# A transformer kernel with routed experts on one Trainium2 core: row transfers, pair rows and weight loads issued at other places

## The chip, the cores and the metric

The kernel runs on one core of a Trainium2 chip. TensorE (PE) multiplies matrices, VectorE (DVE) and ScalarE (ACT) work on rows, GpSimd (POOL) computes small things and issues indirect transfers, SyncE (SP) issues all other transfers. The metric is the device time of one execution in microseconds (us), lower is better.

## The reference

Two layers, each of a cross-attention and a mixture of eight experts, on 16 sequences of 128 tokens with 128 features. Everything is float32.

```python
x = x + jnp.tanh(g_xattn[0]) * _L0_xattn_ref(_layernorm(x, axis=-1), ctx_512, Wq, Wkv, Wo)
x = x + jnp.tanh(g_ffn[0]) * _L0_ffn_ref(_layernorm(x, axis=-1), gate_w, w1, w2)
x = x + jnp.tanh(g_xattn[1]) * _L1_xattn_ref(_layernorm(x, axis=-1), ctx_512, ctx_512, Wq, bq, Wk, bk, Wv, bv, Wo, bo)
x = x + jnp.tanh(g_ffn[1]) * _L1_ffn_ref(_layernorm(x, axis=-1), Wr, br, W1, b1, W2, b2, gamma, beta)
```

The attention has 16 heads of 8 features, 128 queries and 77 keys for each sequence. The feed-forward picks for each token the two experts (128 to 512 to 128 features, gelu in layer 0, relu in layer 1) with the largest gate logits and weights their outputs by a softmax of the two. Layer 1 adds biases and a layer norm with gamma and beta.

## The kernel before

Each engine has its own program, written out by hand; semaphores named in ONE and PAIR tie them together, and each engine goes through its program strictly in the order of the code. A layer has four parts: the attention loop, a tail with the routing, an expert loop of 39 tiles of 128 rows, and what follows.

**The attention loop** runs over steps s = 0 to 17. Sequence b is in flight over several steps: in step s the engines prepare sequence s (normalise, `xn`), make the queries of s-1, take the maxima and exponentials of b2 = s-2, and finish b3 = s-3 (weighted values, division, output projection, residual). Sequences are also handled in pairs, (0,1), (2,3) and so on, named by their second, odd member: for pair b4 = s-4, in odd steps, the rows of the updated x are normalised again for the experts ("pair rows", `xfa`), turned by PE, and give the gate logits; three to five steps later the routing has placed them, and POOL sends each sequence's rows to their two experts by two indirect transfers (`scatter(b, j, (k,))`, k = 0 and 1): sequence j = 0 of pair b8 = s-8 in odd steps, j = 1 of pair b9 = s-9 in even ones. So steps 9 to 15 have two transfers each, and steps 5 and 7 handle a pair without any transfer. 

What a step does, engine by engine, where the change and the prediction touch it (names as in the code and the trace):

- DVE: `maxima(b2)`, two TENSOR_REDUCE mx<-banks that follow PE's four score matmuls in pairs; the parts of the maxima (mxp); `divided(b3)` (RECIPROCAL); statistics of sequence s+2; `residual(b3)`; statistics of a pair (fmv); routing.
- PE: lower scores of b2 (they wait for the second exponential of the step before), values and weights of b3, queries of s-1, the turned maxima, scores of b2 (room,kz) with `less_max` (room,less), the turned xn, `project(b3)`, `turn_rows(b4)` (MATMUL banks<-ident,xfa, an odd step's only, waits for the pair rows), then `upper_scores(b1)` (MATMUL banks<-kz,room 32x324), on which DVE's next maxima wait.
- ACT: queries (q_s), `normed(s)` (xn<-x,rstd, waits for POOL's rstd), a copy of the turned maxima, `normalised(b4)` (xfa<-x,frs, odd steps), four exponentials (`exps`, ACTIVATE room<-banks 128x384), the copy xnT.
- POOL: `deviations(b4)` (frs, odd steps), in layer 1 half of the sum of expert outputs for sequence s+3 (x<-ob,x), the deviations rstd of the next two sequences (even steps), `counted`, and then the step's two scatters.

In layer 0, SP's `load_rest()` issues 256 KB weight loads, two per step, for all four weight tensors: wa1 and wa2 (layer 0's) in steps with sequence 0 to 7, wb1 and wb2 (layer 1's) with 8 to 15, and 15 small loads (`late_rows`) in between. The expert loop's row loads (`load_tiles`) come after that on the same queue.

Of the kernel before, what the change touches and what calls it, by code (L numbers as in the profile page):

```python
# [29 lines left out]
B = 16  # L30
# [6 lines left out]
E = 8  # L37
# [80 lines left out]
def pipeline(eng, n, lead, deep, step):  # L118

    for s in range(n + deep):  # L120
        step(Step(s))


def build(nc, a, out):
    ctx = ExitStack()
    with ctx:  # L126
# [296 lines left out]
        def _(sp):  # L423
            def load(dst, src, key):
                sp.dma_start(dst, src).then_inc(ld[key], 16)
# [13 lines left out]
            def load_rest():  # L439
                w1_, w2_ = a["L0_ffn_w1"], a["L0_ffn_w2"].rearrange("e (c p) d -> e p c d", p=P)  # L440
                w3_, w4_ = a["L1_ffn_W1"].rearrange("e (c p) d -> e p c d", p=P), a["L1_ffn_W2"]
                blocks = lambda w, e: w[:, e * F:(e + 1) * F].rearrange("p (c d) -> p c d", c=FC)
                pieces = ([lambda e=e: load(wa1[:, e * F:(e + 1) * F], w1_[e], "wa1") for e in range(E)]
                          + [lambda e=e: load(blocks(wa2, e), w2_[e], "wa2") for e in range(E)]
                          + [lambda e=e: load(blocks(wb1, e), w3_[e], "wb1") for e in range(E)]
                          + [lambda e=e: load(wb2[:, e * F:(e + 1) * F], w4_[e], "wb2") for e in range(E)])
                def late_rows():
                    with nc.allow_non_contiguous_dma(reason="two biases of 128 numbers, reordered"):
                        for dst, src in LATE:
                            load(dst, src, "w1")  # L450

                for c in range(B):
                    layers[0]["mx"].wait(sp, Step(c))
                    pieces[2 * c]()
                    layers[0]["ex"].wait(sp, Step(c))
                    pieces[2 * c + 1]()
                    if c == B // 2:
                        late_rows()

            def attention():  # L460
                S = layers[1]
# [4 lines left out]
                        sp.dma_start(ob[s.slot(UN)][:, k, :], o_dram[0][k * NTOK + c * T:k * NTOK + (c + 1) * T, :])\  # L466
                            .then_inc(s_ob[s.slot(UN)], 16)

            def load_tiles(l):
                S = layers[l]  # L470
                hear(sp, f"rowsT{l}")
                for r in range(2):
                    sp.wait_ge(s_sc[r], SC_LAYER * (l + 1))
                sp.wait_ge(s_zero, 16 * E)
                row = sp.alloc_register(f"row{l}")

                def tile(t):
                    S["xt"].wait(sp, t.back(UN))
                    apart(sp)
                    S["id"].wait(sp, t.back(UN))  # L480
                    apart(sp)
                    sp.reg_load(row, r_row[0:1, bass.ds(t.at(1), 1)])
                    r = sp.snap(row, min_val=0, max_val=E * REGION - P)
                    sp.dma_start(xg[t.slot(UN)][:, :], xg_dram[bass.ds(r, P), :]).then_inc(s_xg[l][t.slot(UN)], 16)
                pipeline(sp, NT, UN, 0, tile)

            hear(sp, "rows")
            for e in range(E):

                sp.dma_start(xg_dram[e * REGION:e * REGION + P, :], zero_row[:, :]).then_inc(s_zero, 16)  # L490
            load_rest()
            load_tiles(0)
            for r in range(UN):
                sp.wait_ge(s_os[0][r], 16 * len(range(r, NT, UN)))
            attention()
# [22 lines left out]
        def _(pool):  # L518
# [74 lines left out]
            def attention(l):  # L593
# [36 lines left out]

                def step(s):
                    b4, b8, b9 = (s.back(n) for n in (4, 8, 9))
                    if live_pair(b4) and live(s):
                        deviations(b4)
                    if l == 1 and UN <= s.c + 3 < B:
                        n = Step(s.c + 3)
                        pool.wait_ge(s_scaled, n.c - UN + 1)
                        pool.tensor_tensor(x[:, seq(n)], ob[n.slot(UN)][:, 0, :], x[:, seq(n)], ALU.add)\
                            .then_inc(s_first, 1)
# [21 lines left out]
                        pool.tensor_scalar(nq[:, lo:2], q_[:, lo:2], -1.0, None, ALU.mult).then_inc(rs.sem, 1)  # L661
                    if placed(s):
                        counted(placed(s))
                    for b, js in ((b8, (0,)), (b9, (1,))):
                        if live_pair(b) and s.c < B:
                            placed_rows(b)
                            for j in js:
                                scatter(b, j)
                    if s.c == B - 1:
                        scatter(FOURTH.back(2), 1)  # L670
                    if s.c == B:
# [458 lines left out]
        def _(act):  # L1130
# [43 lines left out]
            def attention(l):  # L1174
# [30 lines left out]
                def step(s):  # L1205
                    b1, b2, b3, b4 = (s.back(n) for n in (1, 2, 3, 4))
                    if l == 1 and UN <= s.c + 3 < B:
                        n = Step(s.c + 3)
                        s_ob.wait(act, n)
                        rows0 = ob[n.slot(UN)][:, 0, :]  # L1210
                        act.activation(rows0, rows0, ACT.Identity, scale=w01g[:, 2 * n.c:2 * n.c + 1],
                                       bias=zero_row[:, 0:1]).then_inc(s_scaled, 1)
                    if live(s) and s.c == 1:
                        normed(s)
                    if live(b1):

                        S["q"].wait(act, b1)
                        S["st"].wait(act, b3)
                        if l == 0:
                            ins = act.activation(q_s[b1.slot(2)][:, :], bank[5][:, NC * T:NC * T + P], ACT.Copy, scale=SCALE)  # L1220
                        else:
                            ins = act.activation(q_s[b1.slot(2)][:, :], bank[5][:, NC * T:NC * T + P], ACT.Identity,  # L1222
                                                 scale=SCALE, bias=bqs[:, :])
                        ins.then_inc(S["qe"].sem, 1)
                    if live(s) and s.c != 1:
                        normed(s)
                    if s.c == B + 1:
                        normalised(PRIOR)
                    if live(b2):
                        S["mt"].wait(act, b2)  # L1230
                        S["st"].wait(act, b3)
                        copy(mxs[:, :], bank[3][:, W:W + T // 2].bitcast(BF16)).then_inc(S["mtc"].sem, 1)
                        if live_pair(b4) and live(s):
                            normalised(b4)
                        S["pv"].wait(act, b2.back(2))
                        exps(b2, 2, 1)
                        exps(b2, 3, 2)
                        if live(s):
                            S["t1"].wait(act, s)
                        exps(b2, 0, 3)  # L1240
                        exps(b2, 1, 4)
                    if live(s):
                        S["t1"].wait(act, s)
                        S["q"].wait(act, b1)
                        copy(xnT[:, :], bank[4][:, NC * T:NC * T + P]).then_inc(S["c1"].sem, 1)
                    if live_pair(b4) and live(s):
                        S["t2"].wait(act, b4)
                        copied(b4, bank[7])
# [543 lines left out]
```

## Time and profile before

| | |
|---|---|
| median of 3 runs | 489.41 us (487.96 to 492.49) |
| the profiled execution | 493.38 us, span 491.6 us |
| mean granted PE clock | 0.917 |
| PE busy | 425.2 us, 87% of the span |
| DVE busy | 314.5 us, 64% |
| ACT busy | 230.1 us, 47% |
| POOL busy | 236.9 us, 48% |
| transfers | 32.76 MB, mean 67 GB/s |

The profile comes from one execution; its own time is 4 us above the median, and 1.8 us of it lie around the span. Busy shares are means over stages of different kind: attention of layer 0 runs from about 19 to 123 us, its experts from 159 to 242, attention of layer 1 from 253 to 355, its experts from 382 to 462.

### The profile page before, as it was taken

The numbers are of one execution on the slowest core, as the hardware profiler recorded it, in microseconds if no ns is written. First come the engines' busy times: TensorE is split into PE (matmuls) and PEld (weight loads), VectorE is DVE, ScalarE is ACT, GpSimd is POOL, SyncE is SP. The second block draws the span as 40 slices with busy tenths as digits, with TensorE's granted clock in tenths as the row PEclk, the third lists the DMA queues.
The fourth block names the chain that finished last, engine by engine and source line by source line (L and its number), as shares of the span: only waits on it lengthen the run. The fifth ranks groups of instructions, "written<-read, shape, count | busy, mean of one in ns | idle before, by whom it ended". The sixth has DMA issues, their size and how long they took to land. (4 is left out here: it accounts for less than half of the span.)

```text
span 491.6 us, 16017 instructions
## 1 busy us (share of the span) xinstructions
PE 425.2 (87%) x5480; PEld 335.1 (68%) x5484; DVE 314.5 (64%) x1132; ACT 230.1 (47%) x656; POOL 236.9 (48%) x407
## 2 busy tenths in 40 slices
PE   8899989877778979999889998887889799999963
PEld 4566666654453979999646675554666699989853
DVE  4688866763654676666565888874657556656635
ACT  3556435431271434444224665554326466656614
POOL 7222553553550334444331235656456787854526
PEclk9799987986957999999897999999669999999998
DMA  6233333331211113222120011000021122222163
GB/s 172 56 96 93 100 99 91 110 89 58 82 43 29 52 53 78 70 68 74 40 77 23 24 28 32 24 26 30 24 78 41 47 69 63 75 68 74 45 176 88
DMA packets 45284, 32.76 MB, mean 67 GB/s; under 512 B 7432, under 2 KB 40885, under 8 KB 45205
## 3 DMA queue, kind: packets, MB, share of 16 engines
q1 hardware_dynamic: 40661, 22.12, 17.1%
q0 software_dynamic: 4544, 9.61, 6.1%
q8 instruction: 46, 0.75, 0.6%
q14 instruction: 33, 0.27, 0.2%
HBM read 20.50 MB, written 11.21 MB: 65 GB/s over the span
## 5 line engine op out<-in xcount | busy, mean ns | idle before, releaser
L705 POOL DMA_INDIRECT o_rows<-room,ids x78 | 78.7, 1009 | 78.2 <-issue 38.1
L748 PE MATMUL banks<-room 128*128 128x128 f32 x624 | 83.8, 277 | 5.3 <-DVE room L1662 2.7
L748 PE MATMUL banks<-wa,room 128*128 x624 | 82.9, 276 | 0.2 <-ACT room L1294 0.2
L748 PEld LDWEIGHTS banks<-room 128*128 128x128 f32 x624 | 75.7, 192 | 8.6 <-issue 7.1
L599 POOL DMA_INDIRECT xg_rows<-xfa,slots x64 | 64.2, 1003 | 29.8 <-issue 16.6
L748 PEld LDWEIGHTS banks<-wa,room 128*128 128x128 f32 x624 | 76.1, 192 | 0.7 <-issue 0.6
L1179 ACT ACTIVATE room<-banks 128x384 f32<-128x384 f32 x128 | 52.8, 496 | 29.6 <-PE banks L748 20.7
L1440 DVE TENSOR_REDUCE mx<-banks 128x8 f32<-128x648 f32 x64 | 50.2, 825 | 14.6 <-PE banks L748 14.2
L1294 ACT ACTIVATE room<-banks,b_cols 128x128 f32<-128x128 f32 x156 | 44.6, 369 | 27.8 <-PE banks L748 22.3
L1662 DVE COPY room<-wa 128x512 f32 x78 | 33.7, 433 | 33.0 <-issue 17.4
L748 PE MATMUL banks<-kz,room 32*128 32x324 f32 x256 | 43.5, 547 | 4.9 <-ACT room L1179 4.6
L1134 ACT ACTIVATE room<-banks 128x128 f32<-128x128 f32 (+1 forms) x110 | 30.7, 279 | 28.0 <-PE banks L751 19.9
L1507 DVE RECIPROCAL room<-banks 128x128 f32<-128x128 f32 x32 | 30.5, 952 | 17.6 <-remote 9.5
L748 PE MATMUL banks<-room,kz 32*128 32x128 f32 x768 | 33.2, 305 | 8.8 <-ACT room L1222 4.7
L1289 ACT ACTIVATE room<-banks 128x512 f32<-128x512 f32 x39 | 23.3, 597 | 30.8 <-PE banks L748 29.8
L748 PE MATMUL banks<-room,keep 128*32 128x128 f32 x768 | 33.7, 301 | 3.9 <-issue 3.7
L748 PEld LDWEIGHTS banks<-room,v_s 128*32 128x32 f32 x768 | 23.0, 124 | 20.4 <-ACT room L1179 14.8
L748 PE MATMUL banks<-room,v_s 128*32 128x128 f32 x768 | 34.9, 317 | 2.1 <-DVE x L1516 1.1
L748 PEld LDWEIGHTS banks<-room,kz 32*128 32x128 f32 x768 | 27.4, 202 | 12.3 <-issue 11.2
L748 PE MATMUL banks<-wide 128*128 128x512 bf16 x112 | 31.1, 439 | 2.9 <-POOLq L289 1.4
L748 PEld LDWEIGHTS banks<-room,keep 128*32 128x32 f32 x768 | 25.6, 124 | 6.7 <-issue 6.0
L1516 DVE SCALAR_TENSOR_TENSOR x<-banks,tg,x 128x128 f32<-128x128 f32 x32 | 11.1, 347 | 27.1 <-PE banks L748 20.0
(209 smaller groups left out, 706.9 us busy)
## 6 DMA issues: line engine op xcount, KB each, us to landing
room<-xg_rows SPq DMA_DIRECT2D x78, 68.5 KB
wa<-in_L_ffn_w SPq DMA_DIRECT2D x16, 256.0 KB, 2.7
wb<-in_L_ffn_W SPq DMA_DIRECT2D x16, 256.0 KB
ob<-o_rows SPq DMA_DIRECT2D x32, 64.0 KB, 1.9
wb<-o_rows SPq DMA_DIRECT2D x6, 256.0 KB, 4.7
o_rows<-room,ids POOLq DMA_INDIRECT x78
x<-in_x SPq DMA_DIRECT2D x4, 256.0 KB, 3.6
xg_rows<-xfa,slots POOLq DMA_INDIRECT x64
```

The source lines that it names most:

```text
L599: pool.indirect_dma_start(out=xg_dram, in_=xfa[:, at, :], in_offset=None, out_offset=bass.IndirectOffsetOnAxis(ap=slots[:, at, k:k + 1], a ...
L705: pool.indirect_dma_start(out=o_dram[l], in_=o_sb[t.slot(UN)][:, :], in_offset=None, out_offset=bass.IndirectOffsetOnAxis(ap=ids[t.slot(UN ...
L748: return pe.matmul(out_, lhsT, rhs, start=start, stop=stop)
L1134: return act.activation(out_, in_, ACT.Copy)
L1179: act.activation(probs[b.slot(2)][g][:, :], bank[(4, 5, 0, 1)[g]][0:M, 0:NC * T], ACT.Exp)\
L1289: act.activation(hid[:, :], bk[:, :], func).then_inc(S["act"].sem, FC)
L1294: act.activation(hid[:, c * P:(c + 1) * P], bk[:, c * P:(c + 1) * P], func, bias=b1_cols[:, bass.ds(e4 + c, 1)]).then_inc(S["act"].sem, 1)
L1440: dve.tensor_reduce(mx[r][:, G * g:G * (g + 2)].rearrange("p (i j) -> p i j", i=2), two.rearrange("p i (j k) -> p i j k", j=G), AX.X, ALU. ...
L1507: dve.reciprocal(den[:, :], bank[6][:, T:2 * T]).then_inc(rc.sem, 1)
L1516: dve.scalar_tensor_tensor(x[:, seq(b)], bank[6][:, 2 * T:3 * T], tg[:, l:l + 1], x[:, seq(b)], ALU.mult, ALU.add).then_inc(S["x2"].sem, 1)
L1662: dve.tensor_copy(w1s[s.slot(2)][:, :], wa1[:, bass.ds(e, F)]).then_inc(S["wc"].sem, 1)
```

## The change

Three things move, nothing is added or left out.

1. POOL: a step's two scatters stood at its end. Now the first (k = 0) stands at the step's start and waits for all four score matmuls of b2 (the moment at which DVE's maxima can run through), the second (k = 1) follows the pair's deviations, and everything else of the step (x<-ob,x, rstd, counted) comes behind both.
2. ACT: `normalised(b4)` stood between the copy of the turned maxima and the four exponentials. Now it stands behind them, ahead of the copy xnT.
3. SP: layer 1's 16 weight loads leave the attention loop and are issued in the expert loop of layer 0, one with every second tile from tile 4 on. The 15 small loads come five steps earlier.

```diff
-                for c in range(B):
+                for c in range(8):
                     layers[0]["mx"].wait(sp, Step(c))
                     pieces[2 * c]()
+                    if c == 3:
+                        late_rows()
                     layers[0]["ex"].wait(sp, Step(c))
                     pieces[2 * c + 1]()
-                    if c == B // 2:
-                        late_rows()
+                return later
...
                     sp.dma_start(xg[t.slot(UN)][:, :], xg_dram[bass.ds(r, P), :]).then_inc(s_xg[l][t.slot(UN)], 16)
+                    if UN <= t.c < UN + 2 * len(pieces) and t.c % 2 == 0:
+                        pieces[(t.c - UN) // 2]()
...
                     b4, b8, b9 = (s.back(n) for n in (4, 8, 9))
+                    b2 = s.back(2)
+                    for b, js in ((b8, (0,)), (b9, (1,))):
+                        if live_pair(b) and s.c < B:
+                            placed_rows(b)
+                            S["sc"].wait(pool, b2)
+                            scatter(b, js[0], (0,))
                     if live_pair(b4) and live(s):
                         deviations(b4)
+                    for b, js in ((b8, (0,)), (b9, (1,))):
+                        if live_pair(b) and s.c < B:
+                            scatter(b, js[0], (1,))
...
-                    for b, js in ((b8, (0,)), (b9, (1,))):
-                        if live_pair(b) and s.c < B:
-                            placed_rows(b)
-                            for j in js:
-                                scatter(b, j)
...
-                        if live_pair(b4) and live(s):
-                            normalised(b4)
                         S["pv"].wait(act, b2.back(2))
                         exps(b2, 2, 1)
                         exps(b2, 3, 2)
...
                         exps(b2, 0, 3)
                         exps(b2, 1, 4)
+                    if live_pair(b4) and live(s):
+                        normalised(b4)
```

POOL, layer 0, steps 11 and 12. DMA is a scatter, frs the pair's deviations, rstd those for the next two sequences, cum the counts. Before:

```order
L589 TENSOR_SCALAR frs<-fmv 128x2
L591 TENSOR_TENSOR frs<-frs,mhalf 128x2
L627 TENSOR_TENSOR frs<-fmv,frs 128x2
L629 TENSOR_SCALAR frs<-frs 128x2
L599 DMA xg_rows<-xfa,slots 17408x137 x2
L589 TENSOR_SCALAR rstd<-mv 128x2
L591 TENSOR_TENSOR rstd<-rstd,mhalf 128x2
L659 TENSOR_TENSOR rstd<-mv,rstd 128x2
L661 TENSOR_SCALAR rstd<-rstd 128x2
L608 TENSOR_TENSOR cum<-cum,mb 128x8
L610 TENSOR_TENSOR cum<-cum,mb 128x8
L599 DMA xg_rows<-xfa,slots 17408x137 x2
```

The same place in the changed kernel:

```order
L602 DMA xg_rows<-xfa,slots 17408x137
L592 TENSOR_SCALAR frs<-fmv 128x2
L594 TENSOR_TENSOR frs<-frs,mhalf 128x2
L630 TENSOR_TENSOR frs<-fmv,frs 128x2
L632 TENSOR_SCALAR frs<-frs 128x2
L602 DMA xg_rows<-xfa,slots 17408x137 x3
L592 TENSOR_SCALAR rstd<-mv 128x2
L594 TENSOR_TENSOR rstd<-rstd,mhalf 128x2
L671 TENSOR_TENSOR rstd<-mv,rstd 128x2
L673 TENSOR_SCALAR rstd<-rstd 128x2
L611 TENSOR_TENSOR cum<-cum,mb 128x8
L613 TENSOR_TENSOR cum<-cum,mb 128x8
```

Of the three transfers in a row the first is the odd step's second, the other two are the even step's, and they now stand ahead of rstd.

ACT, layer 0, step 7, from the queries to the queries of step 8; the four 128x384 are the exponentials, xfa the pair rows. Before:

```order
L1220 ACTIVATE room<-banks 128x128
L1190 ACTIVATE xn<-x,rstd 128x128
L1134 ACTIVATE room<-banks 128x128
L1197 ACTIVATE xfa<-x,frs 128x128 x2
L1179 ACTIVATE room<-banks 128x384 x4
L1134 ACTIVATE xnT<-banks 128x128
L1134 ACTIVATE xfT<-banks 128x256
L1220 ACTIVATE room<-banks 128x128
```

The same place in the changed kernel:

```order
L1227 ACTIVATE room<-banks 128x128
L1197 ACTIVATE xn<-x,rstd 128x128
L1141 ACTIVATE room<-banks 128x128
L1186 ACTIVATE room<-banks 128x384 x4
L1204 ACTIVATE xfa<-x,frs 128x128 x2
L1141 ACTIVATE xnT<-banks 128x128
L1141 ACTIVATE xfT<-banks 128x256
L1227 ACTIVATE room<-banks 128x128
```

The pair rows have passed the four exponentials. PE's order is the same in both kernels: what waits for the pair rows there still stands ahead of the upper scores.

## Rows read from the trace of the kernel before

**Rows 1.** Windows: both attention loops; busy time by engine, clock, DMA share, GB/s.

```profile
19.00:123.00 104.00, 92.12 (x1648) 64.00 (x1645) 70.94 (x232) 44.99 (x133) 38.86 (x81) 0.86 0.32 91
...
253.00:355.00 102.00, 85.36 (x1405) 60.06 (x1409) 71.53 (x237) 52.69 (x151) 45.71 (x97) 0.94 0.09 26
```

**Rows 2.** Timeline, layer 1, step 7, a pair without transfers: start, length, engine, line.

```profile
287.07 0.27 ACT L1134 ACTIVATE room<-banks 128x128 bf16<-128x128 bf16 x1
287.23 0.87 ACT L1197 ACTIVATE xfa<-x,frs 128x128 f32<-128x128 f32 x2
...
288.13 1.64 ACT L1179 ACTIVATE room<-banks 128x384 f32<-128x384 f32 x4
...
288.47 0.38 PE L751 MATMUL banks<-ident,xfa 128*128 128x128 f32 x2
...
288.79 1.09 PE L748 MATMUL banks<-kz,room 32*128 32x324 f32 x8
...
290.00 1.56 DVE L1440 TENSOR_REDUCE mx<-banks 128x8 f32<-128x648 f32 x2
```

**Rows 3.** Timeline of ACT, layer 1, step 6: exponentials right after the copy.

```profile
282.75 1.64 ACT L1179 ACTIVATE room<-banks 128x384 f32<-128x384 f32 x4 [0.48 <-PE banks L748]
```

**Rows 4.** Timeline, layer 0, step 5, a pair without transfers.

```profile
37.11 1.64 ACT L1179 ACTIVATE room<-banks 128x384 f32<-128x384 f32 x4
...
38.13 0.83 PE L748 MATMUL banks<-kz,room 32*128 32x324 f32 x8
...
39.08 1.57 DVE L1440 TENSOR_REDUCE mx<-banks 128x8 f32<-128x648 f32 x2 [1.19 <-PE banks L748]
```

**Rows 5.** Timeline, layer 1, step 9, a pair with two transfers.

```profile
297.97 1.08 POOL L599 DMA_INDIRECT xg_rows<-xfa,slots  x1 [0.16 <-issue]
298.37 0.28 ACT L1134 ACTIVATE room<-banks 128x128 bf16<-128x128 bf16 x1
...
299.35 1.08 POOL L599 DMA_INDIRECT xg_rows<-xfa,slots  x1 [0.30 <-issue]
...
300.90 1.64 ACT L1179 ACTIVATE room<-banks 128x384 f32<-128x384 f32 x4 [1.48 <-remote]
...
302.29 1.56 DVE L1440 TENSOR_REDUCE mx<-banks 128x8 f32<-128x648 f32 x2
```

**Rows 6.** Timeline, layer 1, step 10: POOL's sum and rstd, ACT's xn.

```profile
303.43 0.45 POOL L638 TENSOR_TENSOR x<-ob,x 128x128 f32<-128x128 f32 x1 [3.01 <-ACT ob L1211]
...
305.36 0.24 POOL L661 TENSOR_SCALAR rstd<-rstd 128x2 f32<-128x2 f32 x1
...
305.63 0.49 ACT L1190 ACTIVATE xn<-x,rstd 128x128 f32<-128x128 f32 x1 [0.70 <-POOL rstd L661]
```

**Rows 7.** Timeline, layer 0, step 10: maxima and xn.

```profile
61.97 1.57 DVE L1440 TENSOR_REDUCE mx<-banks 128x8 f32<-128x648 f32 x2
...
64.43 0.48 ACT L1190 ACTIVATE xn<-x,rstd 128x128 f32<-128x128 f32 x1
```

**Rows 8.** Timeline of POOL, layer 0: a transfer behind a computing instruction.

```profile
70.89 1.07 POOL L599 DMA_INDIRECT xg_rows<-xfa,slots  x1 [0.48 <-issue]
```

**Rows 9.** Instructions of line 1179 (exponentials): idle ended by "remote", us and times.

```profile
  remote: 8.5, 5
```

**Rows 10.** Timeline, layer 1, after three transfers over PE's values and weights.

```profile
348.15 0.95 POOL L599 DMA_INDIRECT xg_rows<-xfa,slots  x1 [0.30 <-issue]
...
350.04 0.96 DVE L1507 RECIPROCAL room<-banks 128x128 f32<-128x128 f32 x1 [2.74 <-remote]
```

**Rows 11.** Layer 0, step 11: a window with its clock, and its maxima and the next.

```profile
70.00:72.00 2.00, 2.00 (x41) 1.50 (x33) 0.75 (x3) 0.00 (x0) 1.40 (x3) 0.50 0.53 156
...
68.84 1.56 DVE L1440 TENSOR_REDUCE mx<-banks 128x8 f32<-128x648 f32 x2
...
78.67 1.57 DVE L1440 TENSOR_REDUCE mx<-banks 128x8 f32<-128x648 f32 x2 [1.24 <-PE banks L748]
```

**Rows 12.** Transfer issues: a weight load's size, and us to landing.

```profile
wa<-in_L_ffn_w SPq DMA_DIRECT2D x16, 256.0 KB, 2.7
```

More of the change, by code:

```diff
@@ L443, in load_rest @@
                 pieces = ([lambda e=e: load(wa1[:, e * F:(e + 1) * F], w1_[e], "wa1") for e in range(E)]
-                          + [lambda e=e: load(blocks(wa2, e), w2_[e], "wa2") for e in range(E)]
-                          + [lambda e=e: load(blocks(wb1, e), w3_[e], "wb1") for e in range(E)]
-                          + [lambda e=e: load(wb2[:, e * F:(e + 1) * F], w4_[e], "wb2") for e in range(E)])
+                          + [lambda e=e: load(blocks(wa2, e), w2_[e], "wa2") for e in range(E)])
+                later = ([lambda e=e: load(blocks(wb1, e), w3_[e], "wb1") for e in range(E)]
+                         + [lambda e=e: load(wb2[:, e * F:(e + 1) * F], w4_[e], "wb2") for e in range(E)])
                 def late_rows():
@@ L467, in attention, with load_tiles @@
                             .then_inc(s_ob[s.slot(UN)], 16)
-            def load_tiles(l):
+            def load_tiles(l, pieces=()):
                 S = layers[l]
@@ L490, in _ @@
                 sp.dma_start(xg_dram[e * REGION:e * REGION + P, :], zero_row[:, :]).then_inc(s_zero, 16)
-            load_rest()
-            load_tiles(0)
+            later = load_rest()
+            load_tiles(0, later)
             for r in range(UN):
```

## The prediction

> **What bounds the kernel now.** I read the windows by stage first. The two attention loops take 104 and 102 us [rows 1], two fifths of the span, and the moves on POOL and ACT lie in them; the third move puts loads into layer 0's expert loop. In the attention loops no engine is busy all the time (PE 92.12 and 85.36 us, DVE about 71) [rows 1], so the timeline of single steps had to tell what sets a step's length. It is a ring over three engines: DVE's maxima, PE's scores, ACT's exponentials, PE's scores of the next sequence, DVE's maxima again. I take the start of a step's maxima as its mark. In a clean odd step the exponentials start at 288.13, PE turns the pair rows at 288.47, starts the next scores at 288.79, and the next maxima start at 290.00 [rows 2]. What is put into this ring lengthens the step.
>
> The second thing to see is what the transfers do. In step 9 POOL issues one at 297.97 and one at 299.35. ACT's copy ends at 298.65, and the exponentials, which start 0.48 us after the copy where nothing disturbs [rows 3], come at 300.90, after 1.48 us of idle time that ended by "remote" [rows 5]. Five such waits cost 8.5 us [rows 9]. PE's signals reach ACT late while POOL issues transfers. The same is seen at DVE: its reciprocal waits 2.74 us for PE's weights and starts at 350.04, 0.94 us after the last of three transfers ended at 349.10 [rows 10].
>
> **Pair rows behind the exponentials, steps without transfers (5 and 7 of each layer).** What is gained: in step 7 the exponentials can start 0.48 us after the copy's end at 287.34, so at 287.82 instead of 288.13, 0.31 us. What is lost: PE's turn_rows waits for the pair rows and stands ahead of the upper scores. The four exponentials take 1.64; the pair rows take 0.87 and start 0.11 before the instruction ahead of them ends, as they do behind the copy now (287.23 against 287.34) [rows 2]: 287.82 + 1.64 - 0.11 + 0.87 = 290.22. The scores start 0.32 after the turn does [rows 2], so at 290.54 instead of 288.79. The maxima start 0.95 after the scores where they wait for them (38.13 to 39.08) [rows 4]: 291.49 instead of 290.00, +1.5 us. Here ACT's old slack is gone: PE stands for 1.7 us. In layer 0 I let the exponentials stand at 37.11 (a gain is bounded by layer 1's 0.31); pair rows end 2.40 later at 39.51, scores start at 39.83, maxima at 40.78 instead of 39.08 [rows 4]: +1.70. What follows the scores on PE (values, weights, queries) shifts by as much, so the next step doesn't catch up. Four steps: 2 x 1.5 + 2 x 1.7 = **6.4 us**.
>
> **The same with transfers (odd steps 9 to 15).** If the stall goes, the exponentials start at 298.65 + 0.48 = 299.13. Pair rows end 2.40 later at 301.53, scores start at 301.85, maxima at 302.80 instead of 302.29: +0.5. So even where the whole stall of 1.48 us is saved, the pair rows' new place eats it. POOL's deviations start one transfer later (1.08 and the gap of 0.30 behind it [rows 5]), which the exponentials now hide; ahead of them this would have cost ACT the same. The step's second transfer falls close to less_max and the projection, and its signals may still be held: then the stall comes back, up to 1.5 more. In layer 0 the stalls were smaller, since 8.5 us in five waits is both layers' [rows 9], and the loss is between 0.5 and the 1.7 of a clean step; I take 0.9. Step 15, where transfers of two pairs run on each other before and after, I leave at nothing. Three steps each: 3 x 0.5 + 3 x 0.9 = **4.2 us**.
>
> **Transfers ahead of rstd (even steps 10, 12, 14).** Before, POOL did the sum and rstd first and the transfers last. Now the transfers wait for the scores of b2, thus for the maxima's start. In step 10 of layer 1 that is 302.29 [rows 5]. Then 0.48 until the first is issued [rows 8], 1.08, a gap of 0.30, 1.08 [rows 5]: POOL is free at 305.23. The sum x<-ob,x started at 303.43 and so shifts by 1.80, and with it rstd and ACT's xn, which waited for rstd already (305.63, idle 0.70) [rows 6]. On ACT the copy of the turned maxima and the exponentials are queued behind xn, PE's less_max, turn of xn and projection wait for them, and DVE's residual for the projection: the whole ring shifts, +1.80. In layer 0 there is no sum: transfers end 2.94 us after the maxima's start at 61.97, at 64.91, and from the end of the sum to the end of rstd it is 1.72 us (303.88 to 305.60) [rows 6]: xn at 66.63 instead of 64.43 [rows 7], +2.20. Three steps each: 5.4 + 6.6 = 12.0 us. I count three quarters, since in a part of these steps a stall or the slow clock had already held xn or the exponentials: **9.0 us**. The transfers now lie over PE's values and weights, of which [rows 10] shows that DVE's reciprocal is then held; in the even steps this is hidden behind the later xn.
>
> **Weight loads.** In layer 0's experts a 256 KB load needs 2.7 us to land [rows 12] and goes ahead of the next tile's row load on SP's queue. Row loads are issued four tiles ahead, so I take nothing. Bounds: 16 x 2.7 = 43 us, were nothing hidden; on the other side the loads leave the attention loop, where DMA share falls from 0.32 towards layer 1's 0.09 [rows 1]. If they were what keeps layer 0's clock at 0.86 instead of 0.94, then 0.08 x 104 = 8.3 us come back. I take zero: the two loops differ by 2 us, with three and a half times the transfers in layer 0 [rows 1]. The small loads are off every path.
>
> **The sum.** 6.4 + 4.2 + 9.0 = 19.6 us. Against the profiled execution: span 491.6, 1.8 around it, 493.4 + 19.6 = 513.0. That execution is 4.0 above the median of the runs shown, so the median should come to 489.4 + 19.6, about **509 us**.
>
> **Rivals.** (1) *Slower clock.* Layer 0's step 11 had the clock at 0.50, that is 1.2 of 2.4 GHz, and took from 68.84 to 78.67, 9.83 us [rows 11], against 6.87 for step 10 right before it (61.97 to 68.84) [rows 7, 11]: +3.0. With PE standing about 1.7 us longer in most steps, three more such stretches give +9, 518 us. Against it: layer 1's loop has such stalls too, and its mean clock is 0.94 [rows 1]. The Trainium skill says in TensorE: Matmul & The Clock Gate, Part 1, that an idle TensorE falls to the lower of two clocks and a busy one comes back to the higher; the two levels agree with the trace, and by that rule this rival would be nearer than mine.
> (2) *Loads held the clock.* The 8.3 us above come back: 489.4 + 19.6 - 8.3 = 501. For it: layer 1, nearly without loads, has the better clock. Against: the loops' lengths, which differ by 2 us only.
> (3) *Faster: the held signals are the whole price.* If transfers at the maxima's start hold no signal that anyone needs, the 8.5 us [rows 9] go, and PE's new wait costs nothing because DVE is not ready for the next maxima anyway: 481 us. It decides from the point where DVE's own work of an odd step ends later than 291.4 in the frame of [rows 2]; before, it started there at 290.00, so 1.5 us would have to come from somewhere.
> (4) *Nothing.* The stalls' 8.5 us pay for odd steps (10.6), and rstd comes early enough because PE signals late anyway: 489 + 2 to 4.
> (5) *Experts pay.* Each of the 16 loads costs a tile 0.7 us: +11, 520. Against: the row loads' four tiles of lead.
>
> **How the numbers follow.** My forecast, 503 to 515, 0.45; the slower clock 0.15; loads held the clock (496 to 503) 0.17; faster 0.08; nothing 0.08; experts pay 0.07. The range from 495 to 521 leaves out the faster case, the even one, and a little above. A measurement of this kernel tells about 1% from no change, 5 us. Faster by over 1%: 0.08, within: 0.08, slower: 0.84.
>
> **What the profile after would show.** In odd steps the pair rows stand behind the exponentials and PE waits for them with its turn, about 1.7 us; in even steps ACT's xn waits for rstd by 2 us and more from step 10 on, and no longer than before in steps 6 and 8; "remote" waits of the exponentials shrink. From one step's maxima to the next it is 1.5 us longer in steps 5 and 7. If PE doesn't wait for the pair rows, the first term is wrong; if xn doesn't wait, the third; if experts of layer 0 take more than 83 us, the fourth.

## The result and the profile after

The changed kernel takes 525.57 us (median of four runs, 524.08 to 535.8) beside 490.95 us for the kernel before on the same chip (487.96 to 498.6): a ratio of 1.0736, 95% interval 1.0674 to 1.0798, or +35 to +36 us. That is slower, as forecast, but beyond the range (495 to 521). Some executions take over 1.5% more than the fastest of their kernel, mostly at a lower clock, and ratios and intervals leave them out. The profiled execution took 524.23 us, its span is 522.5 us, its mean granted clock 0.854 (before 0.917). The profiled execution of the kernel before lies 2.4 us above the 490.95 and this one 1.3 below its median, so the profiles are 31 us apart and not 35.

Both attention loops by windows, as [rows 1], and one stretch of layer 1; the columns are busy us and instructions of PE, PEld, DVE, ACT, POOL, then clock, DMA share and GB/s:

```profile
19.00:123.00 104.00, 84.50 (x1571) 60.19 (x1570) 67.71 (x213) 43.29 (x127) 37.10 (x77) 0.83 0.20 56
253.00:355.00 102.00, 86.44 (x1114) 58.82 (x1112) 60.88 (x190) 43.27 (x124) 34.75 (x80) 0.73 0.10 27
315.00:369.00 54.00, 47.19 (x520) 33.09 (x524) 27.30 (x97) 18.20 (x52) 19.85 (x40) 0.50 0.05 15
369.00:374.00 5.00, 3.44 (x71) 2.60 (x60) 3.24 (x10) 1.87 (x6) 4.24 (x9) 0.94 0.10 31
```

In the same 102 us of layer 1 PE now gets through 1114 matmuls instead of 1405, and the clock is 0.73 instead of 0.94. (Before, these 102 us hold the whole loop; after, they end in step 13.) For 54 us on end the clock stands at 0.50, which is 1.2 GHz. PE is busy for 47.19 of them and its longest idle time in them is 1.58 us, so "busy" doesn't mean a full clock here: it is slow work with repeated short gaps.

The groups and waits of the page that speak of the moved work (last columns: idle us before the group and what ended most of it):

```profile
L1447 DVE TENSOR_REDUCE mx<-banks 128x8 f32<-128x648 f32 x64 | 50.2, 826 | 45.7 <-PE banks L755 45.3
...
L758 PE MATMUL banks<-ident,xfa 128*128 128x128 f32 x32 | 8.4, 354 | 25.2 <-ACT xfa L1204 23.9
```

and of the kernel before:

```profile
L1440 DVE TENSOR_REDUCE mx<-banks 128x8 f32<-128x648 f32 x64 | 50.2, 825 | 14.6 <-PE banks L748 14.2
```

PE waits 23.9 us for pair rows, and DVE's maxima wait 31 us longer for PE's scores than before, as much as the span has lost (522.5 - 491.6 = 30.9). That is where the ring's delay shows up and not yet its cause, since whatever lengthens the ring on PE or ACT ends in this wait. The waits of the exponentials that ended by "remote" [rows 9] are gone. Layer 1, step 9, as [rows 5] (start, length, engine, line; idle time before it in brackets):

```profile
308.99 1.56 DVE L1447 TENSOR_REDUCE mx<-banks 128x8 f32<-128x648 f32 x2
...
309.76 1.07 POOL L602 DMA_INDIRECT xg_rows<-xfa,slots  x1 [3.68 <-DVE slots L1507]
...
312.71 1.07 POOL L602 DMA_INDIRECT xg_rows<-xfa,slots  x1 [0.17 <-issue]
...
312.91 1.64 ACT L1186 ACTIVATE room<-banks 128x384 f32<-128x384 f32 x4 [0.80 <-PE banks L755]
...
314.41 0.89 ACT L1204 ACTIVATE xfa<-x,frs 128x128 f32<-128x128 f32 x2
...
315.45 0.66 PE L758 MATMUL banks<-ident,xfa 128*128 128x128 f32 x2 [2.04 <-ACT xfa L1204]
316.04 1.46 PE L755 MATMUL banks<-kz,room 32*128 32x324 f32 x8
...
317.63 1.57 DVE L1447 TENSOR_REDUCE mx<-banks 128x8 f32<-128x648 f32 x2 [2.57 <-PE banks L755]
```

The chain is the forecast one: exponentials, pair rows, PE's turn after 2.04 us of idle time, upper scores, maxima. The exponentials start 3.92 us after the step's maxima, before it was 5.07, so here the stall of [rows 5] is mostly gone; but from their start to the next maxima it is now 4.72 us instead of 1.39. From 315 on, the same eight score matmuls take 1.46 us instead of 1.09 [rows 2]. An even step, step 12 of layer 1, as [rows 6]:

```profile
338.12 1.57 DVE L1447 TENSOR_REDUCE mx<-banks 128x8 f32<-128x648 f32 x2 [2.39 <-PE banks L755]
338.92 0.98 POOL L602 DMA_INDIRECT xg_rows<-xfa,slots  x1 [6.15 <-PE banks L755]
340.21 0.96 POOL L602 DMA_INDIRECT xg_rows<-xfa,slots  x1 [0.30 <-issue]
341.19 0.46 POOL L650 TENSOR_TENSOR x<-ob,x 128x128 f32<-128x128 f32 x1
...
343.13 0.24 POOL L673 TENSOR_SCALAR rstd<-rstd 128x2 f32<-128x2 f32 x1
343.40 0.49 ACT L1197 ACTIVATE xn<-x,rstd 128x128 f32<-128x128 f32 x1 [1.18 <-POOL rstd L673]
```

Here POOL issues both transfers ahead of the sum and rstd, and xn waits for rstd, though by 1.18 us and not by the 2 us and more that I had expected: the queries ahead of xn on ACT come late as well, and end only at 342.22. The time at which xn starts, 5.28 us after the maxima, is close to the 5.14 (307.43 - 302.29) that I had worked out for step 10.

Where the span went, by the distance from a step's maxima to the next step's, after less before, both profiled executions:

| steps | layer 0 | layer 1 | sum | forecast |
|---|---|---|---|---|
| 2, 3, 4 | +0.3 | +0.2 | +0.5 | 0 |
| 5, 7 (pair, no transfers) | +4.6 | +4.5 | +9.1 | 6.4 |
| 6, 8 | +0.3 | +1.5 | +1.8 | 0 |
| 9, 11, 13, 15 (pair, transfers) | +4.6 | +10.4 | +15.0 | 4.2 |
| 10, 12, 14 (transfers ahead of rstd) | +1.9 | +8.2 | +10.1 | 9.0 |
| 16 | -4.6 | -0.6 | -5.1 | 0 |

That is 31.5 us; everything outside the loops is within 0.6 of before, layer 0's experts among it. The pair steps with transfers miss the forecast most, and they do so in layer 1, where the clock is slow. One cell needs care: the 9.83 us of step 11 in layer 0 [rows 11] belong to that one execution. e3 below has the same order on POOL, ACT and PE and takes 6.76 us there, so 3 us more of the loss than the +4.6 shows lie in these steps. The table alone can't tell the wait from the clock; the experiments do.

### The profile page after: what moved, and what is told of

It reads as the page before. It is cut to its first block and busy times, and to the rows that moved or that the text cites. A ratio compares the mean times of both kernels' runs of the same rounds, so it can differ in the third digit from the quotient of the medians.

```text
span 522.5 us, 16021 instructions
## 1 busy us (share of the span) xinstructions
PE 443.0 (85%) x5484; PEld 349.8 (67%) x5484; DVE 317.8 (61%) x1132; ACT 231.6 (44%) x656; POOL 237.2 (45%) x407
## 5 line engine op out<-in xcount | busy, mean ns | idle before, releaser
L1447 DVE TENSOR_REDUCE mx<-banks 128x8 f32<-128x648 f32 x64 | 50.2, 826 | 45.7 <-PE banks L755 45.3
L755 PE MATMUL banks<-room,kz 32*128 32x128 f32 x768 | 35.0, 317 | 11.0 <-ACT room L1229 5.8
L755 PEld LDWEIGHTS banks<-room,v_s 128*32 128x32 f32 x768 | 26.3, 139 | 24.6 <-issue 15.7
L755 PE MATMUL banks<-room,v_s 128*32 128x128 f32 x768 | 40.5, 356 | 2.4 <-issue 2.4
L755 PE MATMUL banks<-kz,room 32*128 32x324 f32 x256 | 39.6, 632 | 0.0
L755 PE MATMUL banks<-room,keep 128*32 128x128 f32 x768 | 38.2, 341 | 1.6 <-issue 1.5
L755 PEld LDWEIGHTS banks<-room,kz 32*128 32x128 f32 x768 | 28.9, 212 | 15.7 <-issue 15.2
L755 PEld LDWEIGHTS banks<-room,keep 128*32 128x32 f32 x768 | 30.1, 143 | 4.4 <-issue 2.3
L758 PE MATMUL banks<-ident,xfa 128*128 128x128 f32 x32 | 8.4, 354 | 25.2 <-ACT xfa L1204 23.9
```

Source lines behind the costliest of these rows:

```text
L755: return pe.matmul(out_, lhsT, rhs, start=start, stop=stop)
L758: return pe.transpose(out_, in_, idn[0:n, 0:n])
L1447: dve.tensor_reduce(mx[r][:, G * g:G * (g + 2)].rearrange("p (i j) -> p i j", i=2), two.rearrange("p i (j k) -> p i j k", j=G), AX.X, ALU. ...
```

## Experiments

Ratios are against the kernel before on the same chip, with the 95% interval; "us" is the ratio's excess times the median of before. Runs with the same median of before ran on the same chip, the others on different ones. The chips differ: the kernel before took 491.6 to 492.8 us on three of them and 442.4 and 445.2 on two. I call them the slower and the faster chips. The expectations were written in us of the slower chips; where a run fell on a faster one, only its ratio can be held against them.

| | edit | before | ratio (95%) | us |
|---|---|---|---|---|
| e1 | before + ACT move | 492.7 | 1.0611 (1.0545 to 1.0677) | +30.1 |
| e2 | before + POOL move | 492.7 | 1.0122 (1.0057 to 1.0187) | +6.0 |
| e3 | before + SP move | 492.7 | 0.998 (0.9935 to 1.0025) | -1.0 |
| e4 | after, turn behind upper scores | 492.7 | 1.047 (1.0413 to 1.0526) | +23.2 |
| e8 | after + filler in PE's wait | 442.41 | 1.1151 (1.1085 to 1.1217) | +50.9 |
| e9 | after, turn a step later | 442.41 | 1.0673 (1.0592 to 1.0753) | +29.8 |
| e10 | before + ACT move, turn a step later | 442.41 | 1.0337 (1.0265 to 1.0409) | +14.9 |
| e12 | before + ACT move + filler | 442.41 | 1.0456 (1.0382 to 1.0529) | +20.2 |
| c2 | after | 445.23 | 1.1501 (1.1375 to 1.1627) | +66.8 |
| c3 | before + ACT move | 445.23 | 1.1081 (1.0964 to 1.1199) | +48.1 |
| c4 | after, turn a step later | 445.23 | 1.0766 (1.0682 to 1.085) | +34.1 |
| e14 | before + POOL move | 492.78 | 1.0145 (1.0053 to 1.0238) | +7.1 |
| e15 | POOL move, but sum and rstd first | 492.78 | 0.9894 (0.9772 to 1.0016) | -5.2 |
| e16 | before + ACT move + filler | 492.78 | 1.0441 (1.033 to 1.0551) | +21.7 |
| e17 | before + filler, PE not waiting | 492.78 | 1.0119 (1.0021 to 1.0218) | +5.9 |
| e18 | e15 again, 12 executions | 491.58 | 1.0003 (0.9938 to 1.0068) | +0.1 |
| e19 | e15 + SP move, 12 executions | 491.58 | 1.0036 (0.9991 to 1.0081) | +1.8 |

**The three moves apart.** Each kernel is the one before with one part of the diff; e1, the pair rows:

```diff
-                        if live_pair(b4) and live(s):
-                            normalised(b4)
                         S["pv"].wait(act, b2.back(2))
...
+                    if live_pair(b4) and live(s):
+                        normalised(b4)
```

> The kernel before with one of the three moves: the pair rows behind the four exponentials on ACT. The changed kernel took 31 to 35 us more than before, all of it in the two attention loops, and its TensorE clock was at half for 54.6 us in a row in layer 1. Theory A (the pair rows' place opens a wait of about 2 us on PE in every odd step, and the clock falls because PE stands more): most of the loss is here, 510 to 520 us, PE waits for the pair rows in all odd steps, and the granted clock of the loops is lower than before. Theory B (the transfers' place on POOL is the cost, by late rstd and held signals): 495 us or less. The prediction's working gives 489 + 6.4 + 4.2 = 500.

> The kernel before with only POOL's move: the two transfers of a step at its start, ahead of rstd, with the pair rows where they were, ahead of the exponentials. Theory A: 9 us for the six even steps with late rstd, and some for the deviations, which are now one transfer (1.4 us) later and on which the exponentials wait here, less stalls that go: 492 to 505 us, clock near that of before. Theory B: 510 us and more.

> The kernel before with only SP's move: layer 1's 16 weight loads in layer 0's expert loop. Theories A and B both say no change, 487 to 493 us; layer 0's expert loop as long as before. If the loads in the attention loop held its clock, 481 us.

The ACT move alone brings +30.1 of the 35 us, the POOL move 6.0, the SP move nothing. They add up (35.1). The first two terms of my sum, 10.6 together, stand for 30.1, and e1's 523.7 us lie above even theory A's 520; third and fourth are in order as nets.

**PE's turn out of the way.** e4 is the changed kernel with two calls on PE exchanged:

```diff
+                    if live(b1) and b1.c > 0:
+                        upper_scores(b1)
                     if live_pair(b4) and live(s):
...
                         turn_rows(b4, bank[7])
-                    if live(b1) and b1.c > 0:
-                        upper_scores(b1)
```

> The changed kernel with one edit on PE: turn_rows behind the upper scores instead of ahead of them, so that PE has the scores to do while ACT still makes the pair rows, and the next maxima don't wait for the pair rows. Theory A: the wait leaves the ring, 14 steps x about 2 us and the clock come back: 490 to 500 us. Theory B: 518 us or more, since the transfers stay where they are.

+23.2 us of some 35, so a third of the loss comes back: 517.4 us, where theory A had said 490 to 500. That looked like theory B (518 or more), but the timeline shows why the edit couldn't work. Timeline of PE and of DVE, layer 1, from step 5 into step 6 (the first row is the upper scores, the third the lower ones):

```profile
284.01 0.81 PE L755 MATMUL banks<-kz,room 32*128 32x324 f32 x4
286.02 0.44 PE L758 MATMUL banks<-ident,xfa 128*128 128x128 f32 x2 [1.20 <-ACT xfa L1204]
286.39 0.81 PE L755 MATMUL banks<-kz,room 32*128 32x324 f32 x4
...
284.96 0.83 DVE L1447 TENSOR_REDUCE mx<-banks 128x8 f32<-128x648 f32 x1 [0.49 <-PE banks L755]
287.28 0.83 DVE L1447 TENSOR_REDUCE mx<-banks 128x8 f32<-128x648 f32 x1 [1.48 <-PE banks L755]
```

The first half of the maxima starts in time; the lower scores are still behind the turn, and the second half waits for them. The wait had moved by half a step's scores. So e9 puts the turn behind the next step's lower scores, and e10 does it with the ACT move alone. On the same chip as these two, e12 leaves the turn where it is and fills PE's wait with work that nobody reads, 24 matmuls of bf16 into an unused part of a bank; e8 is that in the changed kernel. The filler doesn't make the pair rows come earlier, it only keeps PE busy until they come:

```diff
+                        unread(bank[7][:, 384:512], 24)
                         turn_rows(b4, bank[7])
```

> The changed kernel with turn_rows moved on PE behind the next step's lower scores, so that neither half of the maxima has the pair rows ahead of it. Behind the upper scores alone it gave back only 8 us (517), since the second half of the maxima still stood behind it. Theory A (PE's wait for the pair rows is the largest part of the loss): about 500 us, what POOL's move costs alone, and no wait on xfa. Theory C (something else of ACT's move costs, the later xnT, queries and the later sum on POOL): 510 us and more.

> The kernel before with the pair rows behind the exponentials (which alone took 523 us) and turn_rows behind the next step's lower scores. Theory A: the whole loss of 31 us goes, 487 to 494 us. Theory C: 505 us and more.

> The kernel before with the pair rows behind the exponentials and 24 additional matmuls ahead of turn_rows, as in the run on the changed kernel. Theory A1: 515 us or less, from 523, clock 0.90 or more. Theory A2: 522 to 530.

> The changed kernel with 24 additional 128x128 bf16 matmuls on PE right ahead of turn_rows, in a part of PSUM that nobody reads, in each of the odd steps 5 to 15: PE works while it would stand for the pair rows. They take about 1.3 us at full clock and 2.6 at half, and the wait is about 2 us. Theory A1 (a good part of the loss is the clock, which falls because PE stands): the time falls by 8 us or more against the changed kernel, to 518 or less, and the granted clock rises from 0.85 to 0.89 or more. Theory A2 (the wait in the ring is all, the clock follows and costs little): 523 to 530 us.

e12 costs 20.2 us at a clock of 0.965. Timeline of DVE, layer 1, maxima that open steps 8, 9 and 10, and the windows of both loops:

```profile
271.10 1.57 DVE L1441 TENSOR_REDUCE mx<-banks 128x8 f32<-128x648 f32 x2 [1.82 <-PE banks L748]
276.51 1.56 DVE L1441 TENSOR_REDUCE mx<-banks 128x8 f32<-128x648 f32 x2
283.92 1.57 DVE L1441 TENSOR_REDUCE mx<-banks 128x8 f32<-128x648 f32 x2 [1.37 <-PE banks L748]
```

```profile
19.00:123.00 104.00, 93.27 (x1918) 68.08 (x1916) 78.11 (x261) 51.68 (x146) 48.67 (x95) 1.00 0.36 102
253.00:355.00 102.00, 86.80 (x1491) 65.53 (x1490) 75.11 (x274) 54.25 (x145) 54.88 (x102) 1.00 0.13 38
```

With the clock at full in both loops the pair step 9 still takes 7.4 us and the even step ahead of it 5.4. In layer 0 the pair steps 5 to 13 take 7.2 to 7.5 us, with and without transfers alike. That is the wait by itself.

The 29.8 us of e9 (66.8 for the changed kernel on the other faster chip, below) fit theory A. e10 fits it only in part: 14.9 us stay, where the whole loss was to go. e8, at 50.9, is 15.9 below the changed kernel on that other chip, but its clock is only 0.89 and 0.87 in the two loops, and PE stands in the even steps too (2.29 us in step 10 of layer 0, for what ACT does behind the late xn).

**The same chip for all four.** These settle what a faster chip makes of the kernels.

> The kernel before once more, for its profile on the chip of this comparison: the second chip ran it in 442 us where the first took 490, so every edit has to be compared with the kernels of the same chip. If the difference between the chips is the granted clock and the length of stalls, the steps without transfers are as long on both and the clock is higher on the faster one.

> The changed kernel, as a control beside the next two. Theories A and A1 expect the ratio to before of 1.07 or a little more; if the clock held half of the loss on the first chip and this is a chip with the higher clock, the ratio is lower, 1.05.

> Only the pair rows behind the exponentials, as a control. Theory A: the ratio of the changed kernel less 0.01 to 0.03. With 24 additional matmuls in PE's wait this was 1.046 on the second chip; if the wait drew the clock down there, it is 1.06 here without them (theory A1), else 1.04 or less (A2).

> The changed kernel with turn_rows behind the next step's lower scores, a second time, now beside the changed kernel itself. Theory A: at least half of the changed kernel's loss is gone. Theory C: less than a third.

c1, the unchanged kernel, took 440.46 us, span 438.7 us, clock 0.966. In layer 1, steps 12 and 13, with two transfers each:

```profile
277.05 1.56 DVE L1440 TENSOR_REDUCE mx<-banks 128x8 f32<-128x648 f32 x2
...
280.88 1.07 POOL L599 DMA_INDIRECT xg_rows<-xfa,slots  x1 [0.52 <-DVE rk L1487]
281.09 1.64 ACT L1179 ACTIVATE room<-banks 128x384 f32<-128x384 f32 x4 [0.48 <-PE banks L748]
282.25 0.97 POOL L599 DMA_INDIRECT xg_rows<-xfa,slots  x1 [0.30 <-issue]
...
282.94 1.56 DVE L1440 TENSOR_REDUCE mx<-banks 128x8 f32<-128x648 f32 x2
...
285.39 1.07 POOL L599 DMA_INDIRECT xg_rows<-xfa,slots  x1 [0.47 <-issue]
286.47 1.64 ACT L1179 ACTIVATE room<-banks 128x384 f32<-128x384 f32 x4
```

The exponentials start 0.48 us behind the copy or at once while POOL issues transfers; in [rows 5] they wait 1.48 us. All pair steps of layer 0 from 5 to 13 take 5.4 to 5.8 us here, with transfers or without. As expected of c1, the steps 5 to 8, without transfers, are as long as on the slower chip (5.66, 5.52, 5.44 and 5.62 us in layer 0, there 5.65, 5.53, 5.43 and 5.63). So the stall that I let the ACT move win back isn't in this program as such. Against these steps e12's 7.46, 7.18, 7.18, 7.29 and 7.22 are +1.80, +1.74, +1.74, +1.80 and +1.41. All twelve pair steps of both layers are 22.1 us longer than in c1, and the even steps of layer 1 1.7 shorter, which makes 20.4 us, close to the 20.2 that e12 measures. On this chip the ACT move costs 48.1 us, the whole change 66.8. Both are far above what was expected of these controls (ratios of 1.06 and of 1.05 to 1.07): the expectation that a chip with the higher clock loses less was wrong. Yet PE waits for the pair rows as long as on the other (waits of c2: us, times, longest):

```profile
PE banks L758 <- ACT xfa L1204: 23.0, 12, 2.0
```

So it isn't the wait that has grown but the work around it. Step 8 of layer 0 in c2 has no pair rows, no transfers and nothing that was moved, and its clock is 0.50 from end to end (the step's two maxima, and its window as in the result):

```profile
53.26 1.57 DVE L1447 TENSOR_REDUCE mx<-banks 128x8 f32<-128x648 f32 x2 [2.69 <-PE banks L755]
62.51 1.57 DVE L1447 TENSOR_REDUCE mx<-banks 128x8 f32<-128x648 f32 x2 [1.23 <-PE banks L755]
53.26:62.51 9.25, 9.03 (x127) 6.78 (x124) 5.42 (x18) 2.63 (x8) 0.40 (x2) 0.50 0.14 40
```

It takes 9.25 us, in c1 on the same chip at a clock of 1.00 it takes 5.62. The step follows a pair step in which PE had stood for 1.77 us. In c2's four steps 6 and 8 this comes to 5.6 us over c1.

Turned a step later, the change costs 34.1 (c4) and 29.8 (e9) instead of 66.8, and the ACT move 14.9 (e10) instead of 48.1. c4 gives back 32.7 of 66.8 us, 49%, about the half that theory A asked for. What remains in e10 is the turn itself, which then waits in the even steps: in layer 0, steps 8 to 12, they take 6.48 us and the pair steps 5.35.

**POOL's order and the filler's price on a slower chip.** e14 is e2 again. In e15 the even steps' transfers also wait for the scores, but stand behind the sum and rstd:

```diff
-                    for b, js in ((b8, (0,)), (b9, (1,))):
+                    for b, js in ((b8, (0,)),):
...
+                    if live_pair(b9) and s.c < B:
+                        placed_rows(b9)
+                        S["sc"].wait(pool, b2)
+                        scatter(b9, 1)
```

> The kernel before with only POOL's move, a second time, beside the next kernel. On the first chip it took 8 us more than before, where the transfers of before already stalled PE's signals. On a chip where before runs without those stalls there is nothing for the move to save: the predicted 11 us of the six even steps (rstd late by 1.8 or 2.2 us) and 1.4 us in each odd step with transfers for the later deviations, 18 to 24 us in all.

> The kernel before with POOL's move, but in the even steps the sum x<-ob,x and rstd stay ahead of the two transfers; the odd steps as in the changed kernel. If late rstd is what the move costs in the even steps (theory A), this is 9 to 12 us faster than the run beside it. If the held signals during PE's values and weights cost it (theory B), the two agree within 3 us.

e14 timeline, layer 1, step 10, POOL and ACT:

```profile
302.98 0.99 POOL L599 DMA_INDIRECT xg_rows<-xfa,slots  x1 [1.65 <-PE banks L752]
304.27 0.96 POOL L599 DMA_INDIRECT xg_rows<-xfa,slots  x1 [0.30 <-issue]
...
305.82 0.37 ACT L1226 ACTIVATE room<-banks,bqs 128x128 f32<-128x128 f32 x1 [2.98 <-remote]
307.52 0.49 ACT L1194 ACTIVATE xn<-x,rstd 128x128 f32<-128x128 f32 x1 [1.33 <-POOL rstd L670]
```

e15 at the same place:

```profile
300.21 0.37 ACT L1230 ACTIVATE room<-banks,bqs 128x128 f32<-128x128 f32 x1 [1.21 <-PE banks L756]
301.28 0.49 ACT L1198 ACTIVATE xn<-x,rstd 128x128 f32<-128x128 f32 x1 [0.71 <-POOL rstd L670]
...
301.75 1.18 POOL L599 DMA_INDIRECT xg_rows<-xfa,slots  x1 [0.50 <-DVE rk L1495]
303.24 0.97 POOL L599 DMA_INDIRECT xg_rows<-xfa,slots  x1 [0.30 <-issue]
```

In e14 this step takes 9.92 us, in e15 5.79. The queries of e14 come late, after 2.98 us ended by "remote", but they end at 306.19 and xn then waits another 1.33 us, so what sets xn's start is the late rstd. The two kernels are 7.1 + 5.2 = 12.3 us apart, give or take 7 by their intervals, as theory A said (9 to 12; B: within 3), and in the profiled executions the even steps 10, 12 and 14 of both layers of e14 are longer by 11.7 in sum. e14 fell on a slower chip, so its 18 to 24 us for a chip without stalls stay untested by it. e16 is e12 on this chip, e17 the same filler in the kernel before, where PE has no such wait.

> Only the pair rows behind the exponentials, with 24 additional matmuls in PE's wait, a second time: on the fast chips it took 22 us more than before, against 50 us for the same move without them, but in two comparisons. Theory A1: again 20 to 24 us over before on a fast chip, 25 or less on the slow one (31 without them).

> The kernel before with the same 24 matmuls ahead of turn_rows, where PE does not wait: they lengthen each of the 12 odd steps by up to their 1.3 us and leave the clock alone. Theory A1 (work in the ring costs its length, idle time in the ring costs its length and the clock): 12 to 18 us over before, clock as before. If additional work as such draws the clock up or down, it differs.

The filler costs 5.9 us where PE isn't idle (1.0 to 10.7 by the interval, less than the 12 to 18 expected; it adds 1.3 us to a clean pair step of layer 0, but the even steps of layer 1 get shorter). In PE's idle it gives back time: +21.7 instead of e1's +30.1 here, and +20.2 (e12) instead of +48.1 (c3) on the faster chips, both differences give or take 6 us. Each of these pairs lies on two chips whose times for the kernel before agree within 0.7%; no chip ran both halves of a pair.

**A better version?** e15's 0.9894 was the only ratio below 1 by over 1%, with an interval that reaches 1.0016.

> The kernel before with POOL's move in the odd steps and, in the even ones, sum and rstd ahead of the two transfers, a second time with more rounds: it took 0.989 of before on the slow chip. If the earlier first transfer relieves the stalls that only the slow chip has, the ratio is 0.99 there and 1.00 to 1.01 on a fast one, where there is no stall to save and the deviations come 1.4 us later.

> The same with layer 1's weight loads in layer 0's expert loop as in the changed kernel. Alone that move changed nothing on the slow chip (0.998). Both theories: as the run beside it, within 1%.

With more executions it is 1.0003 on a slower chip, where 0.99 was expected if the stalls were relieved, and with the SP move 1.0036. Neither beats the kernel before.

## Why the prediction was right in sign and too low

**First and second term (6.4 + 4.2 us; the ACT move measured 30.1, and 20 to 22 with the filler).** The mechanism was right: PE's turn waits for the pair rows, ahead of the upper scores. In a clean step at full clock (e12 against c1) it costs 1.7 to 1.8 us in layer 0, as worked out, and 1.9 to 2.2 in layer 1, where I had 1.5: the 0.31 us by which the exponentials were to start earlier did not come, they start 3.64 us after the maxima of step 7 in both kernels.

The step that failed is "even where the whole stall of 1.48 us is saved, the pair rows' new place eats it", with 0.5 and 0.9 for steps 9 to 13 and nothing for step 15: 4.2 us, where the changed kernel's profile has +15.0. It took all of the stall as saved and the rest of the step at full clock. Step 9 of layer 1, forecast at +0.5, is +2.18: the exponentials come 1.15 us earlier and not 1.77, and from them to the next maxima it takes 4.72 us and not 3.67 (2.40 + 0.32 + 0.95). The same 4.72 stand in five of the six steps 9, 11 and 13, each of them partly or wholly at a clock of 0.50; at full clock it is 3.8 (step 5). With the ACT move alone there was nothing saved at all: in e16 the exponentials of layer 1's pair steps 9 to 15 still come after 1.7 to 2.5 us of idle time. And on a faster chip, where there is no stall to save, all twelve pair steps lose 1.4 to 2.2 us.

**The rival "slower clock" (chance 0.15, +9 us).** This is the second failed step, and lies behind about half of the first miss (five steps by 1.05 us, of 10.8): I took the clock as an alternative and put it at nothing in the sum, while it came on top of everything. Filling PE's wait gives back 30.1 - 21.7 = 8.4 us net on the slower chips, near the 9 that I had priced, and 48.1 - 20.2 = 27.9 on the faster. That the 9 comes out is in part luck: I had it from three more stretches like step 11 of layer 0, and e3, with the old order on POOL and ACT, runs that step in 6.76 us instead of 9.83. In the forecast I spoke against the rival with layer 1's mean clock of 0.94; after the change layer 1 is the worse layer (0.73), with 54 us on end at 0.50. The Trainium skill's rule in TensorE: Matmul & The Clock Gate, Part 1 (an idle TensorE falls to the lower clock) stood behind that rival, and the runs agree with it in direction: e12 differs from the plain ACT move, which ran on another chip, only in that PE has work while it waits, and its clock is 1.00 in both loops.

**Third term (9.0 us).** Late rstd came as worked out: in the changed kernel xn starts 4.73 to 4.74 us after the maxima in layer 0 and 4.75 to 5.40 in layer 1, where I had 4.66 and 5.14. e14 less e15 is 12.3 us, against 12.0 in full and 9.0 as taken. The net of the POOL move is 6 to 7 us on a slower chip: against the profile before, e14's even steps 10 to 14 take 14.0 us more, its steps 9, 11, 13, 15 and 16 together 6.5 less. (About 3 of these 6.5 are again step 11 of layer 0, 9.83 us before and 6.65 in e14, where e3 with POOL's old order has 6.76.) On a faster chip the move costs more: e8 less e12, which differ by the POOL and the SP moves, is 30.7 us, e9 less e10 14.9, c2 less c3 18.7. In e8 the even steps 10 and 12 of layer 0 take 9.38 and 9.43 us against 5.63 in e12, +3.8 where I had worked out +2.2. ACT's xn of step 10, in e8 and in e12:

```profile
70.93 0.49 ACT L1198 ACTIVATE xn<-x,rstd 128x128 f32<-128x128 f32 x1 [2.69 <-POOL rstd L673]
...
65.62 0.48 ACT L1191 ACTIVATE xn<-x,rstd 128x128 f32<-128x128 f32 x1
```

It starts 4.74 us after the maxima in e8, as I had it, but in e12 1.95 after them and not the 2.46 of [rows 7], so it shifts by 2.8; the other 1.0 lies behind xn, in a step whose clock is 0.80 instead of 1.00. Held signals have no part in this, since no wait of e8 ends by "remote". I had counted the shift from a step that was late already, and again left out the clock.

**Fourth term (0).** Right: 0.998 (0.9935 to 1.0025) for e3, and layer 0's experts are unchanged. The rivals "loads held the clock" (-8.3) and "experts pay" (+11) are both out.

**The sum again** for a slower chip, from measured parts: 30.1 for the ACT move, of which the filler can give back 8.4, 6.0 for POOL, -1.0 for SP, 35.1 us; the change measured 1.0736 x 490.95, +36.1. For a faster one it is 20.2 + 27.9 + 18.7 = 66.8, which closes by construction, the last two being differences against c3; only the 20.2 is checked apart. The filler's own price is in the 21.7 and the 20.2, and the clock isn't full in e16 (0.91 and 0.92 in the loops), so on the slower chips the split between wait and clock is rough. The rivals "faster" and "nothing" needed a PE that nobody waits for; DVE's maxima wait 45.3 us for it.

**Open.** Why signals from PE reach ACT late beside transfers on some chips and not on others; none of the kernels separates it from the chip. That the gap between e8 and e12 is twice that between e9 and e10 is explained by half: the profiled executions are 30.7 and 19.4 us apart, of which the six even steps make 20.6 and 12.6. With the turn a step later xn of e10's step 10 (layer 0) already starts 3.08 us after the maxima, so late rstd shifts it by 1.5 us instead of 2.8. What granted clock a given pattern of short waits brings is not shown either: c2 and the changed kernel's profile run the same step at 0.50 in one and at 0.91 in the other (step 8 of layer 0).

## What to carry to other kernels

When an instruction moves back on one engine, look up where its reader stands in the next engine's queue: the delay is paid there, by everything behind the reader, and here in each of twelve steps. A repeated short wait on PE is to be priced twice, once as time and once as clock; here the second part was the larger one on the chips that had run at 0.97 before (27.9 against 20.2 us). A saving that rests on a stall seen in one trace belongs in the range and not in the sum, until a second run shows the stall again; so does a price taken from one slow step.

## What the runs showed of the hardware

- The same kernel takes 440 to 452 us on two chips and 483 to 499 us on the others. The faster ones ran it at a granted clock of 0.94 to 0.97, the slower at 0.88 to 0.93, and no profile from the faster ones has a wait that ended by "remote". The same change costs 7% on one kind and 15% on the other.
- PE's granted clock stayed at 0.50 for 54 us while PE was busy for 47.19 of them and never idle for more than 1.58 us.
- A step without any moved work took 9.25 us at a clock of 0.50 and 5.62 at 1.00, on the same chip (c2 and c1).
- Work that nobody reads made a kernel faster: with 24 small matmuls in PE's wait the ACT move costs +20.2 us instead of +48.1, and +21.7 instead of +30.1 on the slower chips.
- One of the five executions of e1 took 1243 us; it is left out of the ratio and was not explained.
